# In the source stage VectorE adds the rows of P before it compares the next pair's one-hots

## The reference

```
edge_index = jnp.stack([src, dst])
h = jnp.maximum(_layernorm(x, axis=-1), 0.0)
x = x + _L0_gnn_ref(h, edge_index, L0_gnn_W, L0_gnn_att_src, L0_gnn_att_dst, L0_gnn_bias)
h = jnp.maximum(_layernorm(x, axis=-1), 0.0)
x = x + _L1_gnn_ref(h, edge_index, edge_attr_64, L1_gnn_W1, L1_gnn_b1, L1_gnn_W2, L1_gnn_b2)
...
        row = edge_index[0]
        col = edge_index[1]
        msg = jnp.concatenate([x[row], x[col], edge_attr], axis=-1)
        h = jax.nn.relu(msg @ W1 + b1)
        msg_out = h @ W2 + b2
        out = jax.ops.segment_sum(msg_out, row, num_segments=x.shape[0])
```

## Time and profile before

| | |
|---|---|
| median of three runs | 5693.36 us (5691.43 to 5695.14) |
| profiled execution | 5693.23 us |
| its span | 5691.4 us |
| TensorE matmuls busy | 5079.6 us (89%) |
| TensorE weight loads busy | 4021.1 us (71%) |
| VectorE busy | 3961.3 us (70%) |
| ScalarE busy | 2970.2 us (52%) |
| GpSimd busy | 3874.4 us (68%) |
| L1366, 856 times | 467.2 us, 546 ns each |
| L1358, 1712 times | 374.5 us (270 ns each) |

### The profile page before, as it was taken

The page is one execution under the profiler, slowest core; times in us unless marked ns, Lnnn a source line. Parts: engine busy times, 40 slices in busy tenths (PEclk is TensorE's granted clock), DMA queues, the critical chain, the costliest instruction groups (busy, mean ns, idle before and its releaser), DMA issues.

```text
span 5691.4 us, 159502 instructions
## 1 busy us (share of the span) xinstructions
PE 5079.6 (89%) x33692; PEld 4021.1 (71%) x33693; DVE 3961.3 (70%) x14408; ACT 2970.2 (52%) x8485; POOL 3874.4 (68%) x3713
## 2 busy tenths in 40 slices
PE   4788888888888886999999999999997999999999
PEld 3677777777777774676666667666665887777787
DVE  6777878878887886555555555545545888888887
ACT  3566666666666663333333333333224777777776
POOL 4777777777777774677777777777776555555553
PEclk6888988888888887999999999999998999999999
DMA  4422222222222234998888888888886998999997
GB/s 110 164 54 52 54 53 53 53 53 53 53 53 54 53 107 138 283 273 266 264 261 258 264 262 261 264 260 260 260 262 185 222 223 219 216 218 220 219 222 190
DMA packets 859992, 994.46 MB, mean 175 GB/s; under 512 B 307993, under 2 KB 663225, under 8 KB 859776
## 3 DMA queue, kind: packets, MB, share of 16 engines
q1 hardware_dynamic: 662496, 610.19, 39.4%
q0 software_dynamic: 190592, 379.87, 23.7%
q10 hardware_dynamic: 6816, 3.38, 0.2%
HBM read 728.41 MB, written 264.62 MB: 174 GB/s over the span
## 4 chain that ended last, share of the span: by engine, by line
PE 57%; issue 11%; POOL 10%; DMA 9%; DVE 8%; DVEq 3%; ACT 2%; POOLq 0%; ACTq 0%; SPq 0%
PE bank L1705 13%; PE bank L1538 10%; PE bank L1628 8%; PE bank L1630 7%; PE bank L1695 7%; DMA xr<-arena 6%; POOL xr L547 5%; POOL arena L499 4%; PE bank L1464 2%; DMA arena<-h_tab,arena 2%; DVE arena L1055 2%; DVE arena L945 2%; PE bank L1618 1%; PE bank L1686 1%; DVE arena L1035 1%
## 5 line engine op out<-in xcount | busy, mean ns | idle before, releaser
L499 POOL DMA_INDIRECT arena<-h_tab,arena x1612 | 1560.4, 968 | 545.8 <-issue 405.6
L547 POOL DMA_INDIRECT xr<-arena x1612 | 1569.6, 974 | 511.8 <-issue 358.2
L1538 PE MATMUL bank<-arena 128*128 128x136 f32 x6448 | 1317.0, 333 | 73.7 <-DVE arena L1055 9.4
L719 ACT ACTIVATE arena<-bank 128x256 f32<-128x256 f32 x1612 | 593.9, 385 | 1388.4 <-PE bank L1630 963.7
L1628 PE MATMUL bank<-arena 128*128 128x256 f32 x3224 | 1023.2, 399 | 91.4 <-ACT arena L719 45.1
L1538 PEld LDWEIGHTS bank<-arena 128*128 128x128 f32 x6448 | 987.1, 215 | 158.4 <-DVE arena L1055 60.8
L561 POOL DMA_INDIRECT arena<-p_tab,arena x428 | 670.2, 1566 | 628.8 <-DMA arena<-p_tab,arena 503.4
L626 ACT ACTIVATE arena<-bank 128x256 bf16<-128x256 bf16 x1612 | 615.3, 382 | 799.1 <-PE bank L1464 714.6
L1630 PE MATMUL bank<-arena 128*128 128x256 f32 x3224 | 970.9, 383 | 0.0
L1705 PE MATMUL bank<-arena 128*128 128x257 f32 x3424 | 899.2, 385 | 7.3 <-issue 3.2
L1055 DVE TENSOR_TENSOR arena<-arena,bank 128x272 f32 x1612 | 694.6, 431 | 184.9 <-PE bank L1538 154.1
(11 more groups left out here) (255 smaller groups left out, 6481.6 us busy)
## 6 DMA issues: line engine op xcount, KB each, us to landing
arena<-xr SPq DMA_DIRECT2D x428, 520.0 KB
arena<-q_tab SPq DMA_DIRECT2D x1612, 128.0 KB
arena<-in_edge_attr SPq DMA_DIRECT2D x61, 832.0 KB
arena<-rel_tab SPq DMA_DIRECT2D x124, 224.0 KB
arena<-h_tab,arena POOLq DMA_INDIRECT x1612
xr<-arena POOLq DMA_INDIRECT x1612
arena<-rel_tab SPq DMA_DIRECT2D x124, 192.0 KB
xr<-arena SPq DMA_DIRECT2D x26, 520.0 KB
```

The lines of the kernel that those rows point to most:

```text
L499: pool.indirect_dma_start(G[:, q, t, :], None, h_tab, bass.IndirectOffsetOnAxis(ap=idx[:, q, t:t + 1], axis=0)).then_inc(sem(f"gath{q}"), 16)
L547: pool.indirect_dma_start(xr, bass.IndirectOffsetOnAxis(ap=pos[:, q, t:t + 1], axis=0), Rb[:, t, :], None).then_inc(sem(f"scat{m}"), 16)
L1538: last = pe.matmul(PSB[3 + t % 2][:, k * H * MW:(k + 1) * H * MW], OH[:, (t + 2 * q) % 4, k * P:(k + 1) * P], flat(msg[:, t, :, :]), start ...
```

## The change

In `sources`, VectorE's loop over the pairs of a turn, the call of `add_r` moves from behind `hotp` to before it. Nothing else changes; the same instructions run with the same operands and the same waits.

```diff
             def sources(i, first=False, last=False):
                 regs = pair_bins(ENG.DVE, pbrow, SB * i, SB)
                 for m in range(SB):
+                    if not (first and m < 2):
+                        add_r(SB * i + m - 2, (m - 2) % SB, first)
                     if m < SB - 1:
                         hotp(i, m + 1, first)
                     else:
                         if not last:
                             hotp(i + 1, 0, False)
-                    if not (first and m < 2):
-                        add_r(SB * i + m - 2, (m - 2) % SB, first)
                     if not (first and m < 4):
                         add_up(SB * i + m - 4, (m - 4) % SB, regs[m])
```

## The result

The changed kernel took 5722.38 us (median of five, 5712.68 to 5731.95) against 5693.36 for the kernel before: a ratio of 1.0048, 95% interval 1.0037 to 1.0059. It is 0.5% slower, where 14 us less were forecast, and outside the range. The profiled execution took 5721.9 us, span 5720.1.

What follows compares the result with a forecast made beforehand. TensorE was taken to bound the stage, other engines counting only where it waits for them. Terms 12 + 0 + 3 + 0 + 0.5 - 1.5 gave 14 us: 5693 - 14 = 5679 us, range 5667 to 5696.

Steps and rivals of the forecast that it cites:

- The forecast gain of odd steps: Odd steps: the addition moves into VectorE's wait for the xr load, so TensorE waits less; 12 us gained, bounds 5.5 and 15.4.
- the 9.9 us before L1705: TensorE's waits at the segment sum in 41 even steps, recovered only if the relu also comes forward; 9.9 us.
- 12 of 15.4: Gain taken for odd steps, 12 us, from 15.4 us of TensorE waits behind addition or relu in 41 even steps.
- the 5.5 before L1695: TensorE's waits at rows of P in 21 even steps, where only the addition stood before it; 5.5 us, called sure.
- The loads: SP's xr loads: sooner relus of odd pairs issue loads sooner, so late L1686 shrinks; 0 to +1.8 us, taken 0.5.
- The index behind the addition: Odd steps with the load long landed: index and gather start up to 0.33 us later; taken 0, -3 for the range.
- The turn start: One-hots of pair 1 go behind the wide addition, but the turn start often comes sooner; +3 us, bounds -7.0 and +7.1.
- The even steps: Other even steps: one-hots behind the wide addition still fit, with 0.44 us to spare; 0, -1 for the range.
- The first, the relu tied to the gather: Rival: the relu still waits for the gather, so only 5.5 us and 0 to 3 are gained; 5686 us, chance 0.30.
- The one on the slower side: Rival: one-hots become late at L1686 of each turn's second step; 5695 us, or 5711 with later pairs too; chance 0.08.
- The weighing of the matmul row: Matmuls busy 1271.46 of 1280 us would leave only 8.5 us free; weight loads at 80% were used instead, leaving room for 14.
- the 57 us: TensorE's excess over its undisturbed pattern, 0.5 us a turn in 107 turns; claimed as all any VectorE reordering could take.

Runs made afterwards that it cites:

- e14: Changed kernel with a semaphore of its own for each slot's gathers, so none waits for the gather two sets back: 0.9980 of the kernel before.
- e11: Changed kernel with half a gather, P's rows added to 64 of the 128 rows: 0.9933 of the kernel before.
- e4: Changed kernel without the gather of P's rows, the relu not waiting for it: 5630.3 us, 0.9884 of the kernel before.
- e13: Kernel before, old order, with a semaphore of its own for each slot's gathers: 0.9985 of the kernel before.
- e10: Changed order with six slots for four and a set's indices written one set earlier: 5730.4 us, 1.0055 of the kernel before.
- e17: As e10, plus a semaphore of its own for each slot's gathers: 5663.85 us, 0.9938 of the kernel before.
- e1: Kernel before with the addition moved before the one-hots in odd steps only: 5728.8 us, 1.0054 of the kernel before.
- e2: Kernel before with the addition moved before the one-hots in even steps only: 5688.2 us, 0.9987 of the kernel before.
- e12: Changed kernel with each xr load waiting for one relu more, so issued later: 1.0370 of the kernel before.
- e3: Changed kernel with the old order kept in the first step of each turn: 5716.0 us, 1.0030 of the kernel before.

## Why the prediction was wrong

**The forecast gain of odd steps (12 us)** was rightly read and wrongly booked. The addition did leave the wait (82 to 23 us), and L1695 never again stood behind it. But the 9.9 us before L1705 hung on the relu's other condition. I chose 12 of 15.4 because "201 places name L1366". A wait is put down to the release that came last; how close behind it the second one stood, that row can't say. The packets could: before the change the gather's last packet was 0.82 us ahead of the relu (median), and after it 0.41, with 0.29 the least in any of 412 sets. There was some half a microsecond to win, and no more however early the addition. Of the 15.4 us only the 5.5 before L1695 came back. Counted alike in both traces, and a little more widely than the 9.9, L1705 came 12.1 us late behind its relu in even steps before and 11.4 after; ScalarE's waits for addition and gather together rose from 82.4 to 105.5 us.

**The loads (+0.5 us)** is the step that failed. Loads issued sooner were booked as a small gain and were the loss. What the runs showed in its place: gather two sets back, gather, and load are tied. The next gather starts only when the one two sets back has landed (318 waits); an earlier load runs beside those packets (225 loads of 412 beside over 128 of them, 81 before), both take longer, the next gather starts later, its relu too, and the stage goes at the gathers' pace. With the tie cut (e14), with half the packets (e11) or none (e4), the changed order loses nothing; with it the loss is 22 us in the stage and 29 in the median. That the loss needs the tie is shown: the order costs 0.5% with it and nothing without (e14 against e13), and cutting it takes 1.2% off e10 (e17). That the earlier load is what slows a gather is read from the packets and fits e1, e2 and e12; the one run that moved the load alone, e12, moved it later and too far.

**The index behind the addition (0, at worst -3)** cost nothing that can be seen: the load's last packet to the index was 0.38 us before and 0.40 after.

**The turn start (+3, bounds -7 to +7)** came to 29.6 us of late starts instead of 7.1: -22.5, far beyond the lower bound. This is where most of the loss shows, since VectorE stands still there for its registers (0.64 us above) and has nothing in hand. Its working took for granted that the load of the turn's first pair lands when it did before. The index of that pair came 0.22 us before L1686 of the step before, by the median, and 0.43 after it in the changed kernel. That is the same late load again, and not the order (e3).

**The even steps (0)** were right: with them alone (e2) the stage is 12.8 us shorter, which is a gain that I had not booked at all.

**The rivals.** The first, the relu tied to the gather, named the wait that took over, but priced it as a gain not made (5686). The one on the slower side named the right place, L1686 of the second step, and a wrong cause. None let the gathers set the pace, since I had read GpSimd's waiting for an earlier gather as nobody's concern. This is its row for the stretch of the earlier trace rows:

```profile
POOL arena L561 <- DMA arena<-p_tab,arena: 498.6, 347, 2.6
```

GpSimd's busy time, 664 of 1280 us, seemed to allow that reading. The weighing of the matmul row came out as the Trainium skill (Perfetto Trace Analysis, Identifying the Most-Contended Engine) says: e17 shows 1160.00 of 1160 us busy and is faster per pair (1.458 us) than every kernel that shows less. And the 57 us that were given as all that a reordering could take were at most 37: a turn freed of the gather takes 11.75 us (e4), not 11.56.

## What to carry to other kernels

Before an instruction is moved out of a wait, follow what it releases round to the transfer that starts sooner, and ask what runs on the DMA engines at that moment. A wait between two transfers of one kind, which only a shared semaphore asks for, can set a pace of its own (latency divided by the number in flight), however idle its engine looks; look for it where an engine waits long and regularly for its own earlier work. And a wait's releaser tells who was last, not how far behind it the second was.

## What the runs showed that I had not expected

A gather of 128 rows puts its first packet on the engines 3.5 us after the start of its instruction on GpSimd (median, before) and ends 4.9 us after it; the next but one starts no sooner than 1.02 us after that (median 1.04). So two in flight give one every (4.88 + 1.04) / 2 = 2.96 us, 11.8 us a turn, while TensorE, unhindered, asks for one every 2.94 (11.75 us a turn in e4); the turns of the kernel before took 12.1. In the changed kernel it is (5.08 + 1.04) / 2 = 3.06 us, 12.2 a turn, and its turns took 12.3.

The 1.21 us from index to gather (0.76 with separate semaphores) is no cost of a second wait as such. Where a gather started that late in the kernel before, the gather two sets back had ended 0.16 us behind the end of the index (median), and GpSimd waited for it. Where it had ended at least 0.16 us ahead, the start came after 0.79 us, and so it did, after 0.85, in most sets of e11 and e12, which have both waits. The DMA engines carried the stage's traffic at a busy share of 0.97 and 228 GB/s in e17 with no one waiting for a gather, while at 0.90 and 216 (e10) 275 relus waited: the share says little of how soon a single transfer lands.
